# Fewer, longer waits of GpSimd for stored groups, gathers written out, and all expert weights copied by VectorE

## What is computed

```python
x = x + attn(layernorm(x))                       # 16 heads of 64, softmax over 256 keys
xn = layernorm(x)
probs = sigmoid(xn @ router_w.T + expert_bias)   # 160 experts
top_w, top_idx = top_k(probs, 8)
top_w = 2.5 * top_w / (top_w.sum() + 1e-9)
routed = sum over the 8 of top_w * (silu(xn @ w_gate[e].T) @ w_down[e].T)
shared = silu(xn @ w_gate_shared.T) @ w_down_shared.T
out = x + routed + shared
```

## Time and profile before

| | us |
|---|---|
| median of three runs | 1271.67 |
| profiled execution, its own time | 1268.07 |
| its span | 1266.2 |
| first gather starts | 762.7 |
| last gather ends | 1259.1 |

### The profile page before, as it was taken

How to read it: one execution, slowest core, us unless ns; L and a number is a source line. 1 busy time by engine, 2 the same in 40 slices (tenths; PEclk the granted TensorE clock), 3 DMA queues, 4 the chain that set the end, 5 groups by cost and what they waited for, 6 DMA issues and landing times.

```text
span 1266.2 us, 30672 instructions
## 1 busy us (share of the span) xinstructions
PE 963.0 (76%) x8800; PEld 723.2 (57%) x8800; DVE 735.0 (58%) x2510; ACT 775.7 (61%) x2405; POOL 698.8 (55%) x892
## 2 busy tenths in 40 slices
PE   5999999999999999999996594575655755756600
PEld 4777777777777777777774373353433533434400
DVE  4578887878787878788884373142323413423442
ACT  6888888778787878888875274473433523634500
POOL 2237666666667666766675404424445355354375
PEclk9999999999999999999996696685666756766755
DMA  8536544444422121222223374463434534434321
GB/s 288 226 136 236 213 176 162 166 159 157 162 95 93 58 87 60 95 74 73 93 106 118 126 252 139 120 194 114 145 101 132 152 106 120 154 115 130 109 79 52
DMA packets 75561, 169.99 MB, mean 134 GB/s; under 512 B 13808, under 2 KB 23984, under 8 KB 75504
## 3 DMA queue, kind: packets, MB, share of 16 engines
q1 hardware_dynamic: 56816, 133.63, 30.0%
q0 software_dynamic: 16384, 33.59, 9.3%
q10 hardware_dynamic: 2304, 2.10, 0.5%
HBM read 66.50 MB, written 102.76 MB: 134 GB/s over the span
## 4 chain that ended last, share of the span: by engine, by line
PE 54%; another core or an unknown queue 14%; issue 12%; ACT 7%; DVE 5%; POOL 4%; DMA 2%; ACTq 1%; DVEq 0%; POOLq 0%; SPq 0%
PE psS L433 9%; PE psO L508 9%; PE psT L458 7%; PE psY L424 7%; PE psA L470 4%; PE psVM L424 4%; POOL yg L949 3%; PE psS L619 3%; PE psT L607 3%; DMA block_y<-y_b 2%; PE psO L630 2%; ACT p_sb L730 2%; ACT w_b L791 2%; PE psY L630 1%
## 5 line engine op out<-in xcount | busy, mean ns | idle before, releaser
L949 POOL DMA_INDIRECT yg<-block_y,tok_idx x256 | 246.2, 962 | 289.1 <-issue 159.1
L921 POOL DMA_INDIRECT slot_x<-xn_src,slot_u x240 | 244.6, 1019 | 99.1 <-issue 53.1
L730 ACT ACTIVATE p_sb<-psS,negmax 128x256 f32<-128x256 f32 x512 | 235.8, 475 | 84.7 <-DVE negmax L1278 83.6
L1319 DVE COPY w_b<-w_all 128x192 f32 x497 | 96.5, 259 | 279.5 <-remote 202.6
L883 POOL TENSOR_SCALAR p_sb<-p_sb,rinv 128x256 f32<-128x256 f32 x256 | 137.4, 544 | 134.1 <-DVE rinv L1227 129.5
L1278 DVE TENSOR_REDUCE negmax<-psS 128x2 f32<-128x512 f32 x256 | 163.9, 681 | 28.4 <-PE psS L433 28.2
L508 PE MATMUL psO<-pT_sb,v_sb 128*64 128x256 f32 x1024 | 138.8, 390 | 21.7 <-ACT pT_sb L306 10.8
L433 PE MATMUL psS<-qk_sb 64*128 64x256 f32 x1024 | 145.2, 402 | 2.7 <-ACT p_sb L730 2.3
L306 ACT COPY pT_sb<-psT 128x512 f32<-128x512 f32 x256 | 140.3, 612 | 2.3 <-PE psT L458 2.3
L607 PE MATMUL psT<-ident,xb 128*128 128x128 f32 x416 | 89.9, 351 | 61.7 <-issue 40.6
L458 PE MATMUL psT<-ident,p_sb 128*128 128x128 f32 x1024 | 132.8, 273 | 0.4 <-POOL p_sb L883 0.4
(11 more groups left out here) (172 smaller groups left out, 1984.9 us busy)
## 6 DMA issues: line engine op xcount, KB each, us to landing
block_y<-zero SPq DMA_DIRECT2D x26, 1024.0 KB
xb<-slot_x SPq DMA_DIRECT2D x104, 256.0 KB
block_y<-y_b SPq DMA_DIRECT2D x104, 256.0 KB
slot_x<-zero SPq DMA_DIRECT2D x15, 1024.0 KB
w_all<-in_wgd_dram SPq DMA_DIRECT2D x16, 960.0 KB
slot_x<-zero SPq DMA_DIRECT2D x1, 11264.0 KB, 41.4
yg<-block_y,tok_idx POOLq DMA_INDIRECT x256
slot_x<-xn_src,slot_u POOLq DMA_INDIRECT x240
```

The lines of the kernel that those rows point to most:

```text
L730: act.activation(p_sb[:, (g - 1) % 2, h, qt, :], psS[:, h, qt * SEQ:(qt + 1) * SEQ], ACT.Exp, bias=negmax[:, (g - 1) % 2, h, qt:qt + 1], s ...
L921: pool.indirect_dma_start(slot_x, bass.IndirectOffsetOnAxis(ap=slot_u[:, int(last), i, j:j + 1], axis=0), (xn2 if last else xn2_src)[:, i, ...
L949: pool.indirect_dma_start(yg[:, r, k, :], None, block_y, bass.IndirectOffsetOnAxis(ap=tok_idx[:, par, r, k:k + 1], axis=0)).then_inc(gat[r ...
```

## The change

GpSimd waits for stored groups in front of six tiles, given by `RUNS`: tiles 0, 2, 6, 14, 22 and 28. Each time it waits for all that the last tile of the run needs, so for 24, 32, 48, 64, 76 and 104 stored groups. Before, tile 2 asked for 28, tile 6 for 36, tile 14 for 52, and tile 22 for 68. All 256 gathers are written out without a loop. They take their row numbers from `pos_u` itself, so `tok_idx`, its copies and their semaphore are gone. All waits are for constants.

VectorE copies all eight slices of every group from 7 on. ScalarE copies none from there, and TensorE no longer waits for it there. Groups 0 to 6 stay as they were.

```diff
-W_EARLY, W_LATE = 5, 4
-ACT_EARLY, ACT_LATE = 7, 28
+W_EARLY, ACT_EARLY = 5, 7
+RUNS = [0, 2, 6, 14, 22, SEALED * TB, NT]
         def copied_by_dve(n):
-            if not isinstance(n, int):
-                return W_LATE
-            if n < 2:
-                return 0
-            return W_EARLY if n < ACT_EARLY else GB if n < ACT_LATE else W_LATE
+            if not isinstance(n, int) or n >= ACT_EARLY:
+                return GB
+            return W_EARLY if n > 1 else 0
...
@@ scalar: experts
-                    if share and (early is None or early + 2 < NGRP and copied_by_dve(early + 2) < GB):
+                    if early is not None and copied_by_dve(early + 2) < GB:
                         weights_of((r + 2) % RING, n + 2)
...
@@ gpsimd
-            def slots_of(n, par):
-                pool.tensor_copy(tok_idx[:, par], pos_u[:, bass.ds(n, YR), :]).then_inc(s["idx_cp"], 1)
-            def gather(n, b, par, r):
-                if not isinstance(n, int) or n >= YR:
-                    wait_apart(pool, s["ys_ok"], n - YR + 1)
+            def groups_done(b):
+                for k in range(2):
+                    pool.wait_ge(sty[k], 8 * NGRP if b >= SEALED else 8 * SEQ_BLK // GB * b + 8 * (E + SEQ_BLK) // GB)
+            def gather(n):
+                r = n % YR
+                wait(pool, s["ys_ok"], n - YR + 1)
...
-                if r % TB == 0:
-                    late = isinstance(b, int) and b >= SEALED
-                    for k in range(2):
-                        wait_apart(pool, sty[k], 8 * NGRP if late else 8 * SEQ_BLK // GB * b + 8 * (E + SEQ_BLK) // GB)
                 for k in range(TOPK):
                     pool.indirect_dma_start(yg[:, r, k, :], None, block_y,
-                                            bass.IndirectOffsetOnAxis(ap=tok_idx[:, par, r, k:k + 1], axis=0)).then_inc(gat[r], 16)
-            def gathers(q, par, last):
-                for r in range(YR):
-                    gather(YR * q + r, YR // TB * q + r // TB, par, r)
-                    if r == YR - 1 and not last:
-                        slots_of(YR * q + YR, 1 - par)
-                if not last:
-                    wait_apart(pool, s["idx_cp"], q + 2)
...
+                                            bass.IndirectOffsetOnAxis(ap=pos_u[:, n, k:k + 1], axis=0)).then_inc(gat[r], 16)
+            for first, end in zip(RUNS, RUNS[1:]):
+                groups_done((end - 1) // TB)
+                for n in range(first, end):
+                    gather(n)
```

More of the change, by code:

```diff
@@ L95, in copied_by_dve @@
         def copied_by_dve(n):
-            if not isinstance(n, int):
-                return W_LATE
-            if n < 2:
-                return 0
-            return W_EARLY if n < ACT_EARLY else GB if n < ACT_LATE else W_LATE
-        def act_copies(n):
-            if not isinstance(n, int):
-                return n - (ACT_LATE - ACT_EARLY)
-            return min(n, ACT_EARLY) if n < ACT_LATE else n - (ACT_LATE - ACT_EARLY)
+            if not isinstance(n, int) or n >= ACT_EARLY:
+                return GB
+            return W_EARLY if n > 1 else 0
         held = {}
@@ L258, in build @@
                 w_cp wa_cp xt2_ps xt2_ok g_ps h_ok y_ps y_ok
-                idx_cp sh_ps hs_ok sho_ps shared_ok yw_ok y4_ok y2_ok ys_ok acc_ok""".split():
+                sh_ps hs_ok sho_ps shared_ok yw_ok y4_ok y2_ok ys_ok acc_ok""".split():
             s[name] = sem(name)
@@ L608, in transposes, with gates @@
                 m.then_inc(s["xt2_ps"], 1)
-            def gates(r, n, share=True):
+            def gates(r, n):
                 par = r % 2
@@ L613, in gates @@
                 wait(pe, s["w_cp"], n - 1)
-                if share and copied_by_dve(n) < GB:
-                    pe.wait_ge(s["wa_cp"], act_copies(n) + 1)
+                if copied_by_dve(n) < GB:
+                    pe.wait_ge(s["wa_cp"], n + 1)
                 wait(pe, s["h_ok"], n - 1)
@@ L632, in downs, with experts @@
                 m.then_inc(s["y_ps"], 1)
-            def experts(it, chunk=None, share=True):
+            def experts(it, chunk=None):
                 for r in range(RING):
@@ L651, in experts @@
                         pe.wait_ge(s["p_ok"], 4 * NSTEP)
-                    gates((r - 1) % RING, n - 1, share)
+                    gates((r - 1) % RING, n - 1)
                     if early == 1:
@@ L680, in _ @@
             with pe.Fori(LEAD, COMBINE_FROM - 3) as it:
-                experts(it, share=False)
+                experts(it)
             for it in range(COMBINE_FROM - 3, COMBINE_FROM - 1):
@@ L822, in _ @@
                 experts(it)
-            with act.Fori(LEAD, ACT_LATE // RING - 1) as it:
-                experts(it, share=False)
-            experts(ACT_LATE // RING - 1)
-            with act.Fori(ACT_LATE // RING, COMBINE_FROM - 1) as it:
+            with act.Fori(LEAD, COMBINE_FROM - 1) as it:
                 experts(it)
@@ L930, in _ @@
             pool.wait_ge(s["scat_l"], 16 * (NT - SEALED * TB) * TOPK)
[L932 to L940 removed]
+            def groups_done(b):
[4 more added lines that the diff above has]
+                wait(pool, s["ys_ok"], n - YR + 1)
+                if n == 2:
                     pool.wait_ge(s["wr_ok"], B)
                     pool.wait_ge(s["po_ok"], B)
[L943 to L947 removed]
                 for k in range(TOPK):
                     pool.indirect_dma_start(yg[:, r, k, :], None, block_y,
[L950 to L969 removed]
+                                            bass.IndirectOffsetOnAxis(ap=pos_u[:, n, k:k + 1], axis=0)).then_inc(gat[r], 16)
[3 more added lines that the diff above has]
+                    gather(n)
         @block.vector
@@ L1312, in shared, with weights_of @@
                 dve.tensor_tensor(xr, psT[:, 0, 0:SEQ].rearrange("p (i d) -> p i d", i=TB), xr, ALU.add).then_inc(s["shared_ok"], 1)
-            def weights_of(r, n, first, share=True):
-                chosen_experts = experts_of(dve, n, 0, copied_by_dve(n) if share else GB)
+            def weights_of(r, n, first):
+                chosen_experts = experts_of(dve, n, 0, copied_by_dve(n))
                 if not first:
@@ L1337, in combine, with turn @@
                                   ALU.add).then_inc(s["acc_ok"], 1)
-            def turn(it, chunk=None, share=True):
+            def turn(it, chunk=None):
                 for r in range(RING):
-                    weights_of(r, RING * it + r, False, share)
+                    weights_of(r, RING * it + r, False)
                     if r == 2 and chunk is not None:
@@ L1368, in _ @@
             with dve.Fori(LEAD, COMBINE_FROM - 3) as it:
-                turn(it, share=False)
+                turn(it)
             group(28)
```

11 lines of the change are left out of this document (removed).

## The result

The changed kernel took 1280.57 us (median of 6 runs, 1276.60 to 1284.74), the kernel before beside it 1270.63 us (6 runs, 1269.08 to 1271.88): a ratio of 1.0088, 95% interval 1.0067 to 1.0109. It is slower by 11 us. The forecast was 1267.4, the range ended at 1280, and faster had the larger chance.

The account below looks back on a forecast made before the run. Bound: the sum of gathers and TensorE's work between bursts. Terms -1.9 + 0 + 0 - 5.8 + 3.4 = -4.3 took 1271.67 to 1267.4 us; range 1257 to 1280.

Parts of the forecast that it names:

- The bound: Expert stage: GpSimd's gathers and TensorE's groups nearly take turns, so time is gathers plus TensorE's work between bursts.
- GpSimd's waits: Waits before bursts: up to 7.5 us of GpSimd's time shortened, counted 0 us, bounds -7.5 and +4.
- Row numbers: Eight row-number copies on GpSimd go, two inside bursts and one in the tail: -1.9 us.
- Longer runs: Tiles 2 and 6 wait for more stored groups and come later while TensorE works on: 0, bounds -3 and +3.
- ScalarE relieved: ScalarE loses 4 weight copies in each of 76 groups, so TensorE waits less for it: -5.8 us.
- VectorE's copies: VectorE copies eight slices per group, delaying its sum at burst ends and tile 22's combination: +3.4, bounds +0.7 and +11.6.
- Copies lock gathers out: Rival: gathers ready while VectorE copies start only when the copy ends, +20 us on bursts, 1287 us; chance 0.05.
- VectorE becomes late: Rival: TensorE waits for VectorE's sum at every burst end and tiles come later, +7.9, 1280 us; chance 0.17.
- no change: Rival: ScalarE's relief is half and VectorE's lateness twice the forecast's, +0.8, 1272 us; chance 0.24.

Follow-up runs that it names:

- gathers only: Kernel before with the changed gathers (written out, six waits, row numbers read in place), weights shared as before: 1286.85 us, 1.0117; on the lower level 1050.23 us, 0.9935.
- the fourth set: Kernel before with the changed gathers, weights shared as before, run again on the upper level: 1286.56 us beside 1269.85, ratio 1.0137.
- pauses alone: Changed kernel with about 1 us of idle GpSimd memsets before the second tile of nine bursts (1275.51 us, 1.0015) or first tile of fifteen (1277.70 us, 1.0014).
- the waits at each pair: Changed kernel with GpSimd waiting for stored groups at every second tile again; lower level: 1054.24 us, 0.9972; 1056.37 us, 0.9986; 1056.90 us, 0.9988.
- weights only: Changed kernel with the gathers of before, so VectorE copies all eight slices from group 7: 1268.09 us, 0.9973; on the lower level 1065.01 us, 1.0071.

## Why the prediction was wrong, step by step

**The bound** was read right for the level of the profile: gathers and TensorE take turns, and much of what TensorE waits for in a burst is "issue". Taken as a property of the kernel, it was wrong: on the lower level the two run side by side.

**GpSimd's waits** is the step that failed: "A wait of GpSimd that is shortened starts the next burst sooner, but TensorE then has that much less done when it is slowed, and makes it up behind the burst: about zero", with +4 as the worst. The gathers' part cost 1.2 to 1.4%, 14 to 17 us. The step held the time lost to TensorE equal to the time taken off GpSimd. The traces of gathers only against before show more lost than that: the bursts got 4.1 us shorter in all and the time behind them 24.8 us longer, with 161 fewer matmuls begun inside the bursts (175 in the trace of the fourth set) and 178 more behind them at 8.1 a us. Bursts in the kernel before had room that a mean over windows hid: one with a row-number copy in it had 108 matmuls, the one shown without 71. But the copies are not all of it. The two bursts that lost one account for 78 of the 161, and of the 102 begun in the last of them before its last gather ended 64 come in the first 8 us, ahead of the copy. Why the other bursts begin fewer is open. That pauses alone win some of it back is shown (1.0015 and 1.0014, upper ends 1.0032 and 1.0045, against 1.0088, lower end 1.0067); how, isn't.

**Row numbers**, -1.9: the gaps are gone, as said, but on the upper level TensorE worked in and behind them: in the last such burst 38 matmuls were begun behind its first 8 us, in the changed kernel none. On the lower level the trace of gathers only has no pause left; what that alone is worth wasn't run.

**Longer runs**, 0: right as far as shown. Tiles 2 and 6 came where forecast, gathers only is level with before at tile 5, and on the lower level the waits at each pair stand at 0.9986 against 0.9998, inside the intervals. Undone by itself on the upper level it wasn't run.

**ScalarE relieved and VectorE's copies**, together -5.8 + 3.4 = -2.4: measured -3.4 us (0.9973) on the upper level. The sum is right; that its two terms are isn't shown. TensorE's waits for VectorE's sum went from 6.4 us to 0.4 in the changed kernel and to 14.3, six waits, in the trace of weights only, where +2.7 was forecast, so the near hit is in part luck. On the lower level the part is a loss of 0.7%, by a way the forecast didn't have: on its trace not TensorE waiting for VectorE, but stretched gathers.

**Copies lock gathers out**, chance 0.05: not seen. In the changed kernel the mean from gather to gather is 1.27 us beside copies and 1.25 beside nothing.

The rival "VectorE becomes late" ended at the right time, 1280, for the wrong reason. The range was too narrow above because its bound of +4 for GpSimd's waits came from the clock alone, one transposition at half speed, and left the slow issue out, which was the largest thing on the rows. One sum of the prediction is off: "no change" takes VectorE's lateness twice but adds 5.6 where twice 3.4 is 6.8, so it ends near 1274, not 1272; it changes no chance that mattered here.

## What to carry to other kernels

When a profile shows two engines taking turns for no reason that it names, find out what stops the one before pricing anything at the other: time taken off the faster turn can cost more than it saves, and the thing to look at is inside the turns (matmuls per burst, burst by burst), not their sum. A pause that looks like waste may be where the other engine works; put it back by itself and see. Engines that wait for a signal long after the work it tells of has ended are a row of their own to look for. And a state that the profile names only "issue" may not belong to the kernel at all: the gathers' part was 1.2 to 1.4% slower with it and 0.65% faster without it, so it is worth running both kernels until both levels have been seen.

## What the runs showed of the hardware

The same program took 1270 us or 1057, each level steady over a set of runs (1263 to 1278 and 1053 to 1063). In the expert stage TensorE begins 2 to 5 matmuls in a us beside indirect DMAs on the one, and 11 to 15 on the other. In attention the levels are near: 32 exponentials of ScalarE, one stage, take 41 us and 39. GpSimd's gathers keep their duration (0.96 us mean on the upper, 0.97 on the lower). The DMA packets take the same time on both (q1 30.0% of 1266.2 us and 36.3% of 1053.0, so 380 and 382 us of 16 engines), and the two queues of instructions move the same (25 and 32 packets).

What goes with the upper level is that TensorE's signals come late beside gathers. A count over the semaphore updates of TensorE in the kernel before, tiles 0 to 25, finds 83 of 114 over 0.5 us behind the end of their matmul inside bursts, the longest 20.1 us, and 3 of 145 between bursts; on the lower level none of 263. Those of ScalarE and VectorE that are on record come within 0.02 us on both levels, but for two in bursts whose own records may be missing. The waits say the same: "remote" is the largest entry of VectorE and ScalarE on the upper level (here in the changed kernel's trace from 835 to 1200 us),

```profile
DVE w_b L1289 <- remote: 140.0, 17, 15.9
ACT h_b L766 <- remote: 104.3, 14, 18.5
ACT y_b L775 <- remote: 77.0, 13, 17.8
```

and on the lower level the same kernel has no remote wait from 750 us to the end of the gathers. There the silu starts 0.12 us behind the end of the gate products:

```profile
833.47 0.69 PE L610 MATMUL psS<-xbT,w_b 128*64 128x64 f32 x16
...
834.28 0.38 ACT L766 ACTIVATE h_b<-psS 128x256 f32<-128x256 f32 x1
```

Whether the slow issue and the late signals have one cause, and which, is open. More records of updates are missing on the upper level too (in bursts 57 of ScalarE's 126, on the lower 15 of 323), so a part of the recording itself isn't ruled out. The Trainium skill's "SBUF — State Buffer", section "Who interferes with whom", has TensorE's ports shared with nobody; by it no port is the cause, and no run here shows what is.

A gather can be stretched by VectorE after all, not by copies but by operations with two inputs that follow each other. GpSimd, then VectorE, of gathers only on the lower level:

```profile
806.12 0.95 POOL L945 DMA_INDIRECT yg<-block_y,pos_u  x1 [0.30 <-issue]
807.38 1.86 POOL L945 DMA_INDIRECT yg<-block_y,pos_u  x1 [0.30 <-issue]
809.54 0.94 POOL L945 DMA_INDIRECT yg<-block_y,pos_u  x1 [0.30 <-issue]
```
```profile
807.19 1.23 DVE L1308 TENSOR_TENSOR yg<-yg,wE_res 128x1024 f32<-128x1024 f32 x1 [4.11 <-DMA yg<-block_y,pos_u]
808.45 0.69 DVE L1310 TENSOR_TENSOR yg<-yg 128x512 f32<-128x512 f32 x1
```

The gather of 807.38 should end at 808.33, beside the multiplication. It ends at 809.24, 0.10 us behind the addition. The 31 gathers of that trace that overlap both such operations have a mean of 1.47 us from start to start; 77 beside nothing have 1.25, and 80 beside copies of weights 1.27. The Trainium skill's "SBUF — State Buffer", section "Who interferes with whom", says that a VectorE operation with two inputs in SBUF contends with a GpSimd operation that reads SBUF, and infers that the making of descriptors is spared; the first half agrees with these rows (1.86 us for 0.95), the inference does not.
